# The softmax shift row of a decoder layer carried by DMA instead of by TensorE, and a reordered start of the cross-attention

## The chip, the cores and the metric

The kernel runs on one core of one Trainium2 chip. The metric is the device time of one execution in microseconds. Before the change it is 1358.77 us, the median of 3 runs (1357.2 to 1359.16).

## What is computed

One decoder layer for 8 batches of 512 tokens, width 256, in float32: a chunked linear attention with a norm, a cross-attention with 16 heads of 64 and a norm, and a feed-forward with ternary weights and a norm. The change lies in the cross-attention and in the seam before it.

```python
# first norm: x = layernorm(x + linear_attention(x))
a = einsum('bmhd,bnhd->bhmn', x @ Wq + bq, ctx @ Wk + bk) / sqrt(64)
a = where(key_mask, a, -inf)
a = softmax(a, axis=-1)
o = einsum('bhmn,bnhd->bmhd', a, ctx @ Wv + bv)
x = layernorm(x + o @ Wo + bo)
# then the feed-forward and a third norm
```

The softmax subtracts each query's maximum over the keys. The kernel adds this (negated) maximum to the scores on TensorE, before the exponential.

## The kernel before

Activations lie transposed: channels on the partitions, the 512 tokens of a batch along the free axis. The kernel has three phases that share the five instruction streams. Every wait is a semaphore written out by hand, and every engine runs its stream in order.

**The linear attention** (`linear_attention_phase`) goes through the 8 batches. Its last batch isn't finished there: its norm (`mean_last`, `square_last`, `variance_last`, `deviation_last`, `normalise`, `deviate_last`) is issued from the start of the cross-attention.

**The cross-attention** (`cross_attention_phase`) goes over 8 batches, and in each over 8 pairs of heads, `g = 8*b + p`. In pair `g`, TensorE runs, in this order: for each of 4 tiles of keys `key_scores` (three products of split values, L1253, then the row `shift` times ones, L1255, which adds the negated maximum), and behind each of them `max_scores` of pair `g+1` (L1261: queries on the partitions, so that a maximum over the keys runs along the free axis); `weighted_values` (L1276) and `sums` (L1285); `maxima_to_row(g+1)` (L1267); `keys` and `queries` of pair `g+2` (`split_matmul`, L48 to L50). Behind pair 0 and pair 4 of a batch come the output projections (`project`), behind pair 7 the values of the next batch.

The path of the maxima: VectorE's `negated_maxima` (L1118) makes, for each of 4 tiles of 128 queries and each of 2 heads, one column `nmx` of 128 partitions. `maxima_to_row` turns the columns into rows with 4 matmuls against the identity, into the PSUM bank `ROW`, and ScalarE's `shift_row` (L1004) copies that bank to the SBUF tile `shift`. ScalarE also runs the four exponentials of a pair (L977), the logarithm and exponential of a reciprocal (L990, L992), the copy of the attended values (L984), and the rounding `att_hi`, `k_hi`, `q_hi` (L1000, L1008, L1012). GpSimd adds up the probabilities (L902, L905) and splits the sums (L914 to L919).

SyncE's stream issues all loads and stores of the loop: once per batch, `store` of the batch before, `load_residual`, and `next_load` (inputs, context, masks of the next batch).

**The seam.** VectorE's order is: `finish_y_last`, `normalise(B-2)`, `queries_lo`, masks, `deviate_last`, the sums of the output weight's rows (L1204), `normalise(B-1)`, subtraction of the output weight's means (L1207), the bias, and then the first pair's maxima. TensorE's order is: values of batch 0 in three groups with `mean_last` and `variance_last` between them, then the first pair's four `max_scores`, then `maxima_to_row(0)`, then the loop. GpSimd splits the output weight (L932, L934) before its loop begins.

**The feed-forward** (`ffn_phase`) follows; the change leaves it as it is.

## Time and profile before

| | |
|---|---|
| median of 3 runs | 1358.77 us |
| the profiled execution | 1358.39 us |
| its span, first to last instruction | 1356.5 us |
| mean granted TensorE clock | 0.983 of full speed |
| TensorE busy | 1302.3 us (96%) |
| VectorE busy | 923.3 us (68%) |
| ScalarE busy | 829.8 us (61%) |
| GpSimd busy | 773.2 us (57%) |

The span and the profiled execution's own time differ by 1.9 us, which lies around the instructions. A matmul's recorded duration is longer than the distance to the next one, since they are pipelined; so the distance between starts is what TensorE's time is read from. The busy share of an engine is a mean over three phases with different limits.

### The profile page before, as it was taken

Reading aid. Unit: us, or ns where it says so; the run is one execution under the profiler, and the core shown is the slowest. Engines: PE = TensorE matmul, PEld = TensorE weight load, DVE = VectorE, ACT = ScalarE, POOL = GpSimd, SP = SyncE. Lnnn points to the kernel's source line nnn. Section 1 sums busy time; section 2 is a strip of 40 time slices with the busy share of each in tenths; the row PEclk is TensorE's granted clock in tenths of the full one; section 3 lists DMA queues with packets and bytes.
Section 4 is the critical chain, followed back from the end, with each engine's and each line's share of the span. In section 5 each row is a group of like instructions: output and inputs, shape, how many; then the busy total and the mean of one; then the engine's idle time right before and its main releaser. Section 6 shows DMA issues by size and latency. Waiting matters only on the chain.

```text
span 1356.5 us, 20922 instructions
## 1 busy us (share of the span) xinstructions
PE 1302.3 (96%) x7056; PEld 881.1 (65%) x7056; DVE 923.3 (68%) x1803; ACT 829.8 (61%) x1122; POOL 773.2 (57%) x447
## 2 busy tenths in 40 slices
PE   6999979999999999999999999999999998899995
PEld 4777756657566656666666666657666665577773
DVE  5678776674766676576657656674775678678885
ACT  2354436674766566565757665675666666678983
POOL 3504327885877687667958767694876787300000
PEclk9999989999999999999999999999999999899997
DMA  6311220000100100010010001000100100111100
GB/s 210 108 39 57 80 79 1 1 1 1 65 1 1 64 0 0 0 64 0 0 64 0 0 0 64 0 0 18 46 0 0 63 1 1 40 38 47 46 32 31
DMA packets 25535, 42.85 MB, mean 32 GB/s; under 512 B 3440, under 2 KB 7936, under 8 KB 25488
## 3 DMA queue, kind: packets, MB, share of 16 engines
q1 hardware_dynamic: 24672, 39.10, 8.5%
q0 software_dynamic: 816, 3.15, 0.7%
q8 instruction: 27, 0.44, 0.1%
q14 instruction: 20, 0.16, 0.0%
HBM read 29.66 MB, written 12.58 MB: 31 GB/s over the span
## 4 chain that ended last, share of the span: by engine, by line
PE 91%; DVE 3%; ACT 2%; POOL 2%; issue 1%; DMA 0%; POOLq 0%; SPq 0%; ACTq 0%; DVEq 0%
PE ps L1276 16%; PE ps L1253 14%; PE ps L48 11%; PE ps L50 10%; PE ps L49 10%; PE ps L1255 4%; PE ps L1261 4%; PE ps L1267 3%; PE ps L1309 2%; PE ps L1310 2%; PE ps L1308 2%; PE ps L1625 2%; PE ps L1624 2%; PE ps L1285 2%; PE ps L57 2%; PE ps L721 1%
## 5 line engine op out<-in xcount | busy, mean ns | idle before, releaser
L1118 DVE CUSTOM_DVE_ANT_0 junk<-ps,mask 128x512 bf16<-128x512 f32 x512 | 319.9, 687 | 94.2 <-PE ps L1261 92.8
L977 ACT ACTIVATE prob<-ps,mcol 128x1024 f32<-128x1024 f32 x256 | 281.8, 1116 | 138.2 <-PE ps L1255 134.9
L905 POOL TENSOR_TENSOR acc<-acc,prob 128x1024 f32<-128x1024 f32 x128 | 306.9, 2398 | 11.5
L902 POOL TENSOR_TENSOR acc<-prob 128x1024 f32<-128x1024 f32 x64 | 154.0, 2406 | 227.4 <-ACT prob L977 226.4
L1276 PE MATMUL ps<-prob,v_b 128*64 128x512 f32 x1024 | 244.5, 599 | 0.0
L919 POOL TENSOR_TENSOR acc_lo<-acc,acc_hi 128x1024 f16<-128x1024 f32 x64 | 138.8, 2169 | 5.1
L1276 PEld LDWEIGHTS ps<-prob,v_b 128*64 128x64 f32 x1024 | 67.8, 136 | 107.8 <-issue 73.9
L1253 PE MATMUL ps<-q_hi,k_hi 64*128 64x512 f32 x512 | 115.6, 446 | 4.6 <-DVE rs L226 2.8
L1261 PE MATMUL ps<-k_hi,q_hi 64*128 64x512 f32 x512 | 103.0, 398 | 6.4 <-DVE nmx L1118 5.5
L1255 PE MATMUL ps<-shift,ones_r 64*128 64x512 f32 x512 | 102.7, 395 | 0.0
L1253 PE MATMUL ps<-q_hi,k_lo 64*128 64x512 f32 x512 | 102.6, 395 | 0.0
L1253 PE MATMUL ps<-q_lo,k_hi 64*128 64x512 f32 x512 | 102.5, 395 | 0.0
L1123 DVE TENSOR_TENSOR ps<-ps,recip 128x512 f32<-128x512 f32 x64 | 44.7, 699 | 69.7 <-ACT recip L992 69.2
L984 ACT ACTIVATE pvc<-ps 128x512 f32<-128x512 f32 x64 | 38.3, 599 | 79.2 <-PE ps L1276 79.1
L1253 PEld LDWEIGHTS ps<-q_hi,k_hi 64*128 64x128 f32 x512 | 48.8, 186 | 54.7 <-issue 26.9
L1136 DVE SCALAR_TENSOR_TENSOR att_lo<-ps,bv,att_hi 128x512 fp32r<-128x512 f32 x64 | 48.0, 751 | 52.8 <-ACT att_hi L1000 52.8
L1146 DVE SCALAR_TENSOR_TENSOR q_lo<-ps,bq,q_hi 128x512 fp32r<-128x512 f32 x64 | 48.0, 751 | 39.3 <-ACT q_hi L1012 39.3
L1012 ACT ACTIVATE q_hi<-ps,bq 128x512 fp32r<-128x512 f32 x64 | 44.0, 688 | 41.8 <-PE ps L50 41.8
L1267 PEld LDWEIGHTS ps<-ident,nmx 128*128 128x128 f32 x256 | 33.9, 192 | 53.0 <-issue 53.0
L1018 ACT ACTIVATE v_b<-ps 128x512 f32<-128x512 f32 x64 | 38.2, 598 | 47.9 <-PE ps L50 47.9
L915 POOL CAST acc_hi<-acc 128x1008 f16<-128x1008 f32 x64 | 65.5, 1023 | 0.0
L1261 PEld LDWEIGHTS ps<-k_hi,q_hi 64*128 64x128 f32 x512 | 48.9, 186 | 22.0 <-DVE nmx L1118 7.1
(213 smaller groups left out, 2983.0 us busy)
## 6 DMA issues: line engine op xcount, KB each, us to landing
x_in<-in_xT SPq DMA_DIRECT2D x8, 512.0 KB, 3.7
x_scratch<-x_a SPq DMA_DIRECT2D x8, 512.0 KB, 2.9
raw<-in_cT SPq DMA_DIRECT2D x8, 512.0 KB, 5.7
raw<-x_scratch SPq DMA_DIRECT2D x8, 512.0 KB, 4.9
y<-x_scratch SPq DMA_DIRECT2D x8, 512.0 KB, 3.8
y_scratch<-y SPq DMA_DIRECT2D x8, 512.0 KB, 2.8
y_c<-y_scratch SPq DMA_DIRECT2D x8, 512.0 KB, 4.1
outT<-x SPq DMA_DIRECT2D x8, 512.0 KB, 2.8
```

The costliest lines, as they stand in the source:

```text
L48: pe.matmul(out, lh, rh, start=(i == 0), stop=False)
L49: pe.matmul(out, lh, rl, start=False, stop=False)
L50: mm = pe.matmul(out, ll, rh, start=False, stop=(i == n - 1))
L902: pool.tensor_tensor(total, prob[:, 0], prob[:, 1], ALU.add).then_inc(acc_out, 1)
L905: pool.tensor_tensor(total, total, prob[:, kt], ALU.add).then_inc(acc_out, 1)
L919: pool.tensor_tensor(acc_lo[:], acc[:], acc_hi[:], ALU.subtract).then_inc(sum_lo_out, 1)
L977: act.activation(prob[:, i].rearrange("p h t -> p (h t)"), SCORE[i % 2].rearrange("p h t -> p (h t)"), ACT.Exp, scale=SCALE, bias=mcol[:, ...
L1118: dve.tensor_tensor_reduce(junk[:, t % 2, h], SMAX[t % 2][:, h], mask[:], -1.0, -LOWEST, ALU.add, ALU.min, nmx[:, t, h * DH:h * DH + 1]).t ...
L1253: pe.matmul(banks[:, h], l[OWN[h], par, cols], r[OWN[h], par], start=(n == 0), stop=False)
L1255: mm = pe.matmul(banks[:, h], ones_r[OWN[h], :], shift[OWN[h], :], start=False, stop=True)
L1261: mm = pe.matmul(SMAX[t % 2][:, h], q_hi[OWN[h], par, toks], k_hi[OWN[h], par], start=True, stop=True)
L1276: mm = pe.matmul(PV[OWN[h], :], v[:, kt, cols], prob[:, kt, h, :], start=(kt == 0), stop=(kt == NT - 1))
```

## The change

The first group of edits concerns the maxima's path, in every pair. `maxima_to_row`, `shift_row`, the identity and the bank `ROW` go. `nmx` shrinks to one column per tile and head, doubled by the parity of the pair, and `shift` is doubled as well. SyncE issues 8 DMAs per pair, each from 128 partitions x 4 bytes of `nmx` to 512 contiguous bytes in one partition of `shift`, as soon as the two maxima of a tile are there. TensorE waits for the maxima where `maxima_to_row` stood (the banks that `queries` writes hold scores), and for the DMAs just ahead of the shift's matmuls in the first key tile. SyncE's other loads and stores are spread over the pairs of a batch.

The second group concerns the seam. The first pair's `max_scores` stand among the values and use the banks of the first keys and queries; VectorE takes the first maxima ahead of the last norm, and the output weight's means behind both. The norm's last step is cut in two functions, `root` and `scale_x1`, with the queries' low part between them for batch B-2. GpSimd splits the output weight in two halves, behind pairs 1 and 4 of batch 0, and clears `shift` before its loop.

```diff
+        def maxima_to_rows(g, p):
+            for t in range(NT):
+                sp.wait_ge(nm_out, 8 * g + 2 * t + 2)
+                for h in range(2):
+                    row = shift[h * DH:h * DH + 1, p % 2, t * P:(t + 1) * P]
+                    sp.dma_start(f32(row), f32(nmx[:, p % 2, t, h:h + 1])).then_inc(row_in[p % 2], 16)
+        def batch(b, first, last):
+            for p in range(PAIRS):
+                if not (last and p == PAIRS - 1):
+                    maxima_to_rows(per_pair(b, p) + 1, p + 1)
+                if p == 0 and not last:
+                    load_context(b + 1)
+                if p == 1 and not first:
+                    store(b - 1)
+                if p == 2 and not first:
+                    load_residual(b)
+                if p == 3 and not last:
+                    load_inputs(b + 1)
+                if p == 4 and not last:
+                    next_masks(b + 1)
...
-        def shift_row(g):
-            act.wait_ge(row_ps, g + 1)
-            act.activation(shift[:], ROW, ACT.Copy).then_inc(row_out, 1)
...
-        values_out(0, (0, 1, 2), FIRST_VAL)
+        values_out(0, (0, 1), FIRST_VAL)
         la.square_last()
-        values_out(0, (3, 4, 5), FIRST_VAL)
+        values_out(0, (2, 3, 4), FIRST_VAL)
         la.deviation_last()
-        values_out(0, (6, 7), FIRST_VAL)
-        shift_row(0)
+        values_out(0, (5, 6, 7), FIRST_VAL)
...
         la.finish_y_last()
-        la.normalise(B - 2)
+        la.root(B - 2)
         for g in range(2):
             queries_lo(g, g, FIRST_QUERY[g])
+        la.scale_x1(B - 2)
         prepare_mask(0, True)
         prepare_mask_columns(0, True)
-        la.deviate_last()
+        dve.wait_ge(bo_ps, 1)
+        dve.tensor_tensor(bo[:], ...)
+        la.subtract_mean_last()
+        first_maxima(0)
+        la.sum_squares_last()
+        for t in range(1, NT):
+            first_maxima(t)
+        la.root(B - 1)
+        la.scale_x1(B - 1)
         dve.tensor_reduce(wo_sum[:], wo[:], AX.X, ALU.add).then_inc(wo_centred, 1)
-        la.normalise(B - 1)
         dve.scalar_tensor_tensor(out=wo[:], ...)
-        negated_maxima(0, 0, 0)
         batch(0, True, False)
...
             for n, (l, r) in enumerate(((k_hi, q_hi), (k_lo, q_hi), (k_hi, q_lo))):
                 for h in range(2):
                     pe.matmul(banks[:, h], l[OWN[h], par, cols], r[OWN[h], par], start=(n == 0), stop=False)
+            if kt == 0:
+                pe.wait_ge(row_in[par], 16 * NT * (g - par) + 32 * NT)
             for h in range(2):
-                mm = pe.matmul(banks[:, h], ones_r[OWN[h], :], shift[OWN[h], :], start=False, stop=True)
+                mm = pe.matmul(banks[:, h], ones_r[OWN[h], :], shift[OWN[h], par], start=False, stop=True)
...
-        def maxima_to_row(g):
-            pe.wait_ge(nm_out, 8 * g + 8)
-            for t in range(NT):
-                mm = pe.matmul(ROW[:, t * P:(t + 1) * P], nmx[:, t, :], c["ident"][:], start=True, stop=True)
-            mm.then_inc(row_ps, 1)
...
                 if nxt:
-                    maxima_to_row(g + 1)
+                    pe.wait_ge(nm_out, 8 * g + 16)
...
+        first_max_scores(0)
+        la.mean_last()
         values(0, (0, 1), FIRST_VAL)
-        la.mean_last()
-        values(0, (2, 3, 4), FIRST_VAL)
+        first_max_scores(1)
+        values(0, (2, 3), FIRST_VAL)
         la.variance_last()
-        values(0, (5, 6, 7), FIRST_VAL)
-        for t in range(NT):
-            max_scores(0, 0, t)
-        maxima_to_row(0)
+        values(0, (4,), FIRST_VAL)
+        first_max_scores(2)
+        values(0, (5,), FIRST_VAL)
+        first_max_scores(3)
+        values(0, (6,), FIRST_VAL)
+        values(0, (7,), FIRST_VAL)
+        pe.wait_ge(la.rs_out, 2 * B - 1)
         batch(0, True, False)
```

## Rows read from the trace of the kernel before

**Rows 1.** The page: the chain that ended last, by engine and by line.
```profile
PE 91%; DVE 3%; ACT 2%; POOL 2%; issue 1%; DMA 0%; POOLq 0%; SPq 0%; ACTq 0%; DVEq 0%
PE ps L1276 16%; PE ps L1253 14%; PE ps L48 11%; PE ps L50 10%; PE ps L49 10%; PE ps L1255 4%; PE ps L1261 4%; PE ps L1267 3%; PE ps L1309 2%; PE ps L1310 2%; PE ps L1308 2%; PE ps L1625 2%; PE ps L1624 2%; PE ps L1285 2%; PE ps L57 2%; PE ps L721 1%
```

**Rows 2.** Groups of instructions: shapes, count | busy us, mean ns | idle before.
```profile
L902 POOL TENSOR_TENSOR acc<-prob 128x1024 f32<-128x1024 f32 x64 | 154.0, 2406 | 227.4 <-ACT prob L977 226.4
...
L1004 ACT ACTIVATE shift<-ps 128x512 fp32r<-128x512 f32 x64 | 38.3, 599 | 11.2 <-PE ps L1267 11.2
```

**Rows 3.** Timeline of pair 28: start us, us, engine, line, operation [idle before].
```profile
611.33 0.39 PE L1285 MATMUL ps<-acc_lo,ones_h 128*64 128x512 f16 x2
...
611.54 2.75 PE L1276 MATMUL ps<-prob,v_b 128*64 128x512 f32 x12
...
611.74 0.08 DVE L1118 DVE_READ_ACCUMULATOR2_ANT nmx<- 128x1 fp32r x1
...
614.22 0.66 PE L1267 MATMUL ps<-ident,nmx 128*128 128x128 f32 x4
...
614.72 0.45 PE L48 MATMUL ps<-bc_hi,wk_hi 128*128 128x512 f32 x1
...
615.41 0.68 ACT L1000 ACTIVATE att_hi<-ps,bv 128x512 fp32r<-128x512 f32 x1
...
617.44 2.16 POOL L919 TENSOR_TENSOR acc_lo<-acc,acc_hi 128x1024 f16<-128x1024 f32 x1
...
617.62 0.50 PE L1253 MATMUL ps<-q_hi,k_hi 64*128 64x512 f32 x2
...
617.73 0.69 ACT L1012 ACTIVATE q_hi<-ps,bq 128x512 fp32r<-128x512 f32 x1 [0.67 <-PE ps L50]
...
618.42 0.39 PE L1255 MATMUL ps<-shift,ones_r 64*128 64x512 f32 x2
```

**Rows 4.** Chain that ended last, in order of time: the values of successive pairs.
```profile
624.15 2.57 PE ps L1276 x12
...
641.98 2.58 PE ps L1276 x12
...
666.82 2.58 PE ps L1276 x12
...
690.27 2.58 PE ps L1276 x12
```

**Rows 5.** DMAs: duration on SyncE's queue (ns), issue to landing, SyncE's timeline.
```profile
L853 SPq DMA_DIRECT2D mcol_u<-in_mask_cols x8: 345/364/599, 161.8 to 950.2; - x8
...
DMA to landing us min/median/max: 2.9/5.0/5.7
...
7.53 5.30 SPq L350 DMA_DIRECT2D bT<-in_fast_bT  x1
```

**Rows 6.** Timeline of the seam and of pair 0.
```profile
191.04 0.39 PE L50 MATMUL ps<-wv_hi,bc_lo 128*128 128x512 f32 x1
...
191.29 0.75 DVE L560 SCALAR_TENSOR_TENSOR rs_a<-ps,eps,inv_a 128x512 f32<-128x512 f32 x1 [3.07 <-ACT inv_a L454]
...
193.94 2.28 DVE L1207 SCALAR_TENSOR_TENSOR wo<-wo_sum,wo 128x2048 f32<-128x2048 f32 x1
...
198.26 4.52 POOL L934 TENSOR_TENSOR wo_lo<-wo,wo_hi 128x2048 fp32r<-128x2048 f32 x1
...
203.31 0.79 PE L1253 MATMUL ps<-q_hi,k_hi 64*128 64x512 f32 x2 [0.78 <-ACT shift L1004]
...
204.73 0.66 PE L1255 MATMUL ps<-shift,ones_r 64*128 64x512 f32 x2
...
210.28 3.65 PE L1276 MATMUL ps<-prob,v_b 128*64 128x512 f32 x16
...
214.37 0.45 PE L48 MATMUL ps<-bc_hi,wk_hi 128*128 128x512 f32 x1
```

**Rows 7.** A window of the seam: length, busy us by engine, granted clock, DMA share, GB/s.
```profile
196.00:200.00 4.00, 1.59 (x4) 0.57 (x4) 3.97 (x15) 0.00 (x0) 3.63 (x2) 0.50 0.95 264
```

More of the change, by code:

```diff
@@ L89, in decoder_layer @@
         c["ones_w"] = sb(whole, "ones_w", [P, P], F32)
-        c["ident"] = sb(whole, "ident", [P, P], F32R)
         c["eps"] = sb(whole, "eps", [P, 1], F32)
@@ L374, in _, with store_x1 @@
         sp.dma_start(c["raw"][:, 0], batch_cols(x1_dram, 0)).then_inc(raw_in, 16)
[L376 to L381 removed]
+        def store_x1(b):
+            sp.wait_ge(x1_out, b + 1)
+            sp.dma_start(batch_cols(x1_dram, b), x1[:]).then_inc(stored, 16)
+        la.store_x1 = store_x1
     @block.gpsimd
@@ L806, in cross_attention_phase @@
     junk = sb(ctx, "junk", [P, 2, 2, T], BF16)
-    shift = sb(ctx, "shift", [P, T], F32R)
-    sb(ctx, "spare", [P, DK, T], F32)
+    shift = sb(ctx, "shift", [P, 2, T], F32R)
+    sb(ctx, "spare", [P, T + 2 * P], F32)
     v = sb(ctx, "v_b", [P, NT, HD], F32)
@@ L871, in load_residual, with load_norm @@
             sp.dma_start(y2[:], batch_cols(x1_dram, b)).then_inc(res_in, 16)
+        def load_norm(b):
+            sp.wait_ge(stored, 16 * b + 16)
+            sp.dma_start(f.y2[:, b], batch_cols(y2_dram, b)).then_inc(f.y_in[b], 16)
+        def maxima_to_rows(g, p):
[8 more added lines that the diff above has]
+                    maxima_to_rows(per_pair(b, p) + 1, p + 1)
+                if p == 0 and last:
+                    sp.wait_ge(x_split, B)
+                    sp.wait_ge(c_split, B)
+                    load_norm(0)
+                if p == 0 and not last:
[4 more added lines that the diff above has]
+                    load_residual(b)
+                if p == 3 and last:
+                    load_norm(1)
+                if p == 3 and not last:
+                    load_inputs(b + 1)
+                if p == 4 and not last:
+                    next_masks(b + 1)
         sp.wait_ge(la.f_step, 3 * DK + DK)
         load_masks(0)
-        la.store_last()
-        sp.wait_ge(la.qm_ps, 2 * B)
+        la.store_x1(B - 2)
+        sp.wait_ge(consts, 3)
+        maxima_to_rows(0, 0)
+        la.store_x1(B - 1)
         load_residual(0)
         sp.wait_ge(la.stored, 16 * B)
-        next_load(1)
+        batch(0, True, False)
         with sp.Fori(1, B - 1) as b:
-            store(b - 1)
-            load_residual(b)
-            next_load(b + 1)
-        store(B - 2)
-        load_residual(B - 1)
-        sp.wait_ge(x_split, B)
-        sp.wait_ge(c_split, B)
-        sp.wait_ge(stored, 32)
-        for b in range(2):
-            sp.dma_start(f.y2[:, b], batch_cols(y2_dram, b)).then_inc(f.y_in[b], 16)
+            batch(b, False, False)
+        batch(B - 1, False, True)
         store(B - 1)
@@ L927, in split_c, with split_output_weight @@
             pool.tensor_tensor(c_lo[:], raw_c, f32(c_hi[:]), ALU.subtract).then_inc(c_split, 1)
-        def split_output_weight():
+        def split_output_weight(half):
+            rows = slice(half * HALF, half * HALF + HALF)
             pool.wait_ge(wo_centred, 2)
-            pool.wait_ge(la.y_out, 2 * B)
-            pool.tensor_copy(wo_hi[:], wo[:]).then_inc(wo_split, 1)
-            pool.wait_ge(wo_split, 1)
-            pool.tensor_tensor(wo_lo[:], wo[:], f32(wo_hi[:]), ALU.subtract).then_inc(wo_split, 1)
+            pool.tensor_copy(wo_hi[:, rows], wo[:, rows]).then_inc(wo_split, 1)
+            pool.wait_ge(wo_split, 2 * half + 1)
+            pool.tensor_tensor(wo_lo[:, rows], wo[:, rows], f32(wo_hi[:, rows]), ALU.subtract).then_inc(wo_split, 1)
         def batch(b, first, last):
@@ L945, in batch @@
                 low_sums(g)
+                if first and p in (1, HALF):
+                    split_output_weight(p // HALF)
                 if p == PAIRS - 3 and not last:
@@ L959, in _ @@
         split_x(0)
-        split_output_weight()
+        pool.wait_ge(la.gate_used, B)
+        pool.memset(f32(shift[:]), 0.0).then_inc(consts, 1)
         batch(0, True, False)
@@ L1118, in negated_maxima, with first_maxima @@
                     dve.tensor_tensor_reduce(junk[:, t % 2, h], SMAX[t % 2][:, h], mask[:], -1.0, -LOWEST, ALU.add,
-                                             ALU.min, nmx[:, t, h * DH:h * DH + 1]).then_inc(nm_out, 1)
+                                             ALU.min, nmx[:, p % 2, t, h:h + 1]).then_inc(nm_out, 1)
+        def first_maxima(t):
+            dve.wait_ge(smax_ps, t + 1)
+            for h in range(2):
+                dve.tensor_tensor_reduce(junk[:, t % 2, h], FIRST_SMAX[t % 2][h], mask[:], -1.0, -LOWEST, ALU.add,
+                                         ALU.min, nmx[:, 0, t, h:h + 1]).then_inc(nm_out, 1)
         def reciprocal(g):
@@ L1253, in key_scores, with first_max_scores @@
                     pe.matmul(banks[:, h], l[OWN[h], par, cols], r[OWN[h], par], start=(n == 0), stop=False)
+            if kt == 0:
+                pe.wait_ge(row_in[par], 16 * NT * (g - par) + 32 * NT)
             for h in range(2):
-                mm = pe.matmul(banks[:, h], ones_r[OWN[h], :], shift[OWN[h], :], start=False, stop=True)
+                mm = pe.matmul(banks[:, h], ones_r[OWN[h], :], shift[OWN[h], par], start=False, stop=True)
             mm.then_inc(st_ps, 1)
+        def first_max_scores(t):
+            toks = slice(t * P, (t + 1) * P)
+            for h in range(2):
+                mm = pe.matmul(FIRST_SMAX[t % 2][h], q_hi[OWN[h], 0, toks], k_hi[OWN[h], 0], start=True, stop=True)
+            mm.then_inc(smax_ps, 1)
         def max_scores(g, p, t):
@@ L1299, in project @@
             if first:
-                pe.wait_ge(wo_split, 2)
+                pe.wait_ge(wo_split, 2 * half + 2)
             pe.wait_ge(att_out, PAIRS * b + HALF * half + HALF - 1)
```

67 lines of the change are left out of this document (28 added, 39 removed).

## Prediction

> **What bounds the kernel now.** I read the chain that ended last first. 91% of it is TensorE, and the lines of the loop carry it; L1267, the four matmuls that turn the maxima into a row, has 3% of its own [rows 1]. So TensorE's order is the spine, and an instruction taken out of it is worth its distance on that spine, unless something else then comes late. Next the timeline of one plain pair. Two plain pairs, from values to values, take 24.84 us, so one takes 12.42 us [rows 4]. The starts of its matmuls follow each other with hardly a gap. ScalarE and VectorE follow TensorE: `q_hi` starts after 0.67 us of waiting for it [rows 3]. GpSimd waits 227.4 us in all for the first exponentials [rows 2], and its last sum, done at 619.60, is used by the L1285 that follows the one at 611.33 by a pair, at 623.75: a margin of 4.1 us [rows 3]. Last the seam, the one stretch in the middle of the kernel where TensorE isn't dense: values end at 191.3, `key_scores` starts at 203.31, and in between the granted clock has fallen to the lower of its two levels, 1.2 GHz [rows 6, 7].
>
> **The loop: what goes.** The group of 12 value matmuls starts at 611.54 and lasts 2.75 us, the last of them 0.39 us like its neighbours, so the last one starts at 613.90; the first L1267 comes at 614.22, and the first L48 at 614.72 [rows 3]. With L1267 gone, the keys can take its place at 614.22: 0.50 us saved. The values go at (2.75 - 0.39) / 11 = 0.21 us a matmul and L1267 comes 0.32 us behind the last; if that extra 0.1 us goes too, it is 0.6 us. This is bounded from above, since the two kinds of matmul that then meet never meet in this trace; I take 0.50, as the wait for the maxima still stands between them, as it stands ahead of L1267 now. Pairs 2 to 62 have this pattern, 61 times: 30.5 us, at most 36.6. A lower end of zero has no reason of its own beyond the third rival, below. (Pair 0 and 1 are in the seam's sum. In front of pair 63 no keys follow, and TensorE waits for the second norm; I count nothing.) The ScalarE copy, 64 times 0.60 us [rows 2], is off the path: it takes part in no wait of TensorE except in the seam and ahead of pair 63. I cost its removal at nothing.
>
> **What is late next.** Once TensorE is 0.50 us earlier at the keys, ScalarE's chain must hold. `att_hi` starts at 615.41 and doesn't depend on L1267 but on the sums of the pair before, so it doesn't move by more than the 0.1 us for which the row's copy held it. It ends near 616.0; `k_hi` (0.69 us) ends at 616.7, and `q_hi` would be ready for its input at 617.23, half a microsecond later [rows 3]. So TensorE still leads, with 0.5 us to spare. GpSimd's margin shrinks from 4.1 to 3.6 us. The gain stands.
>
> **The loop: what comes, and who waits.** SyncE issues 8 DMAs a pair. An issue of the same shape of data (128 pieces of 4 bytes, the mask's columns) holds SyncE 0.36 us [rows 5], with the step to the next some 0.5 us, so 4 us a pair of 11.9. The two maxima of a tile come every 1.2 us or more (8 in some 5 us) and take two issues, 1.0 us: SyncE keeps up, barely. The last maximum of pair 28 is read at 611.82, and the row is first used at 618.42, which becomes 617.92 [rows 3]: 6.1 us. The last of the two issues starts some 0.6 us after the maximum. So the row is in time if it lands within 5.5 us of its issue. The nearest row: those mask columns land in 2.9 us at best, 5.0 in the median and 5.7 at worst, and there they stand right behind two loads of 512 KB [rows 5], while the last row DMA of a pair has nothing ahead of it but its sisters. I take 2.9 us, the undisturbed end, which leaves 2.6 us; the other end, 5.7, costs 0.2 us in a plain pair. No row shows a transfer from SBUF to one partition of SBUF; below 2.9 nothing is gained, since the wait is then met anyway. Behind the waiting SyncE stand the loads and stores of the batch. Each is now issued behind the maxima of its pair: the context in pair 0 for a use in pair 5, the residual in pair 2 for pair 4, the inputs in pair 3 for pair 6; at 12 us a pair each has 20 us or more. They cost nothing. The store in pair 1 waits for the projection of pair 0, done by then. The new wait of TensorE has the other three key tiles, and so all exponentials, behind it.
>
> **The seam.** Before, the last norm and the output weight's means end at 196.2 and the maxima follow, so that the row is used at 204.73 [rows 6]. After, I lay the streams out anew. TensorE's values end at 191.3 before; four score steps of some 0.33 us stand ahead of that end: 192.6. The fourth step stands ahead of two values (6 matmuls of 0.23 us each, 2.8 us together), so it ends at 189.8. VectorE takes its two maxima by 191.2, and SyncE issues by 191.8 and the row lands at 194.7 with 2.9 us. So the row is used 10.0 us earlier. But then VectorE has the norm (2.7 us, from 191.2 to 193.9) and twice 2.3 us of output weight (L1207; the reduction over the same tensor taken as long) [rows 6] before it can serve pair 1: 198.6. TensorE stops ahead of pair 1's third score tile until two tiles' first maxima are there, 199.9, then has 1.5 us of scores and the 3.6 us of values as at 210.28, and reaches the keys at 205.1. Before, that was 214.37: 9.3 us, with the L1267 in it. The bounds: if the stops of 1.4 and 2.4 us bring the clock down again, TensorE's 8.7 us of matmuls in pair 0 take up to twice as long, partly under VectorE's work: 4 us less; if everything fits tighter, 10.5. GpSimd's splitting of the output weight moves from a stretch in which it had nothing else into pairs 1 and 4. The subtraction takes 4.52 us for the whole tensor [rows 6], 2.3 for a half, and the copy, which I take at half of that, brings 3.4 us a half: inside the margin of 3.6. With a copy as slow as the subtraction, pair 2 would wait 0.9 us, once.
>
> **The sum.** 30.5 + 9.3 = 39.8 us. The profiled execution took 1358.39 us, of which 1356.5 are the span, so its own forecast is 1318.6; the median of the runs lies 0.4 us above it: 1319.0 us.
>
> **Rivals.** First, the row lands too late (the slower side). If a DMA of 128 four-byte pieces into one partition takes L us instead of 2.9, every plain pair waits L - 5.5 us, and 39 of the pairs are plain; behind the projections a pair lasts 17.8 us and behind the values 23.5 [rows 4], which covers it. At L = 6.5 the whole gain is eaten; at 8.0 the kernel takes 1358.8 - 39.8 + 39 x 2.5 = 1416 us. For it: nothing in the trace shows this shape, and one issue took 5.30 us on SyncE, with a dozen loads outstanding [rows 5]. Against it: the mask columns, as many and as small pieces, landed in 5.7 us behind 1 MB. I give it 8 in 100, and 6 in 100 to a landing between 5.5 and 6.5 us, with times from 1320 to 1358.
>
> Of this the Trainium skill's page "DMA: Bandwidth & Descriptors" (Rules for kernel authors) warns: a last dimension that isn't contiguous becomes one descriptor per element, and a plain DMA with a rearranged access pattern is put at 19 times a hardware transpose. By that rule the shift would be the bottleneck and this rival the case; the mask columns' row speaks for the contrary at 512 bytes in all.
>
> Second, the seam gives little: the row is late or the clock stays at 1.2 GHz through pair 0. Then the seam brings 3 us, the sum 33.5, the time 1325. For it: before, the clock was at 0.50 between 196 and 200, with TensorE busy 1.59 us of 4 [rows 7]. 12 in 100.
>
> Third, another engine takes half of each 0.50 us, since ScalarE has just 0.5 us to spare; it may also be less by itself if the meeting of values and keys costs more than the one that goes. 61 x 0.25 = 15 us less gain: 1334. Against it: the chain laid out above. 8 in 100.
>
> Fourth, nothing measurable: the DMAs' stalls happen to balance. 2 in 100.
>
> **How the numbers follow.** The forecast has 64 in 100; its own range, from the unknown 30.5 to 36.6 us and the seam's 5.3 to 10.5 us, is 1312 to 1323. The range over all reaches to the third rival and no further, 1310 to 1335, and leaves the two cases of a late row out, about 2 in 10. A measurement of this kernel can't tell less than some 0.2% (2.7 us) from no change. Faster: forecast, second and third rival, and most of the half-late row, 0.88; same 0.04; slower 0.08.
>
> **What would show it.** In the trace after, a plain pair takes 11.92 us (11.82 with the 0.6), the keys start 0.3 us behind the last value matmul, and the first L1255 of a pair's scores follows the first six matmuls without idle time. If the first rival holds, that idle time stands there and names the DMA. The row DMAs' landing is under 5.5 us, and SyncE issues each within a microsecond of its maxima. `q_hi` still waits for TensorE. The first `key_scores` starts near 192.6, its row lands near 194.7, and the keys behind pair 0 start near 205, with a granted clock of 1.00. The prediction is wrong if the landing is over 5.5 us, if an engine other than TensorE sets the plain pair, or if the clock drops in the seam.

## The result, and the profile after

The changed kernel takes 1324.14 us (median of 4 runs, 1323.08 to 1327.98). The kernel before took 1357.99 us beside it (4 runs, 1356.68 to 1359.16). The ratio is 0.9757, with a 95% interval from 0.974 to 0.9774: 2.4% faster. The profiled execution took 1323.5 us, with a span of 1321.6 us, 34.9 us less than the span before. The forecast was 1319.0, with a range from 1310 to 1335.

The page of the changed kernel: the busy time of each engine, the DMA packets, the chain by line, and the row DMAs' landing. The chain answers [rows 1]; of [rows 2], GpSimd's wait for the first exponentials is now 219.7 us, and the copy into `shift` is no longer there.

```profile
PE 1270.6 (96%) x6800; PEld 846.9 (64%) x6800; DVE 923.3 (70%) x1802; ACT 792.9 (60%) x1058; POOL 776.1 (59%) x449
...
DMA packets 99118, 43.07 MB, mean 33 GB/s; under 512 B 77152, under 2 KB 81520, under 8 KB 99072
...
PE ps L1310 16%; PE ps L1285 14%; PE ps L48 11%; PE ps L50 10%; PE ps L49 10%; PE ps L1301 4%; PE ps L1289 4%; PE ps L1342 2%; PE ps L1344 2%; PE ps L1343 2%; PE ps L1660 2%; PE ps L1661 2%; PE ps L1319 2%; POOL acc L931 2%; PE ps L716 1%
...
shift<-nmx SPq DMA_DIRECT2D x512, 0.5 KB, 2.0
```

TensorE still carries the chain. The 3% of the row's matmuls (L1267 before) are gone, and no DMA line is in their place: all that DMAs and SyncE have in the chain lies in the first 21 us, at the loads of the start. In the new numbering L1310 is `weighted_values`, L1319 `sums`, L1285 `key_scores`, L1289 the shift's matmuls, L1301 `max_scores`, L1139 the maxima (L1145 those of the first pair), and L883 the row DMAs.

The timeline of a plain pair of the changed kernel, from the values to the sums of the next pair. It answers [rows 3]. Columns: start, duration, engine, line, operation, idle time before.

```profile
592.69 2.75 PE L1310 MATMUL ps<-prob,v_b 128*64 128x512 f32 x12
...
592.88 0.08 DVE L1139 DVE_READ_ACCUMULATOR2_ANT nmx<- 128x1 fp32r x1
...
595.36 0.50 PE L48 MATMUL ps<-bc_hi,wk_hi 128*128 128x512 f32 x1
...
595.70 0.40 PE L49 MATMUL ps<-bc_lo,wk_hi 128*128 128x512 f32 x1
...
596.46 0.69 ACT L1028 ACTIVATE att_hi<-ps,bv 128x512 fp32r<-128x512 f32 x1 [0.39 <-DVE ps L1158]
...
598.29 0.50 PE L1285 MATMUL ps<-q_hi,k_hi 64*128 64x512 f32 x2
...
598.40 0.69 ACT L1036 ACTIVATE q_hi<-ps,bq 128x512 fp32r<-128x512 f32 x1 [0.67 <-PE ps L50]
598.58 2.15 POOL L945 TENSOR_TENSOR acc_lo<-acc,acc_hi 128x1024 f16<-128x1024 f32 x1
...
599.10 0.39 PE L1289 MATMUL ps<-shift,ones_r 64*128 64x512 f32 x2
...
601.23 4.98 SPq L883 DMA_DIRECT2D shift<-nmx  x8
...
604.43 0.39 PE L1319 MATMUL ps<-acc_lo,ones_h 128*64 128x512 f16 x2
```

The keys (L48) now stand where L1267 stood, 2.67 us behind the start of the values. The shift's matmuls (L1289) follow 0.81 us behind the first `key_scores` (598.29 to 599.10), 0.80 us before [rows 3], and name no DMA. `q_hi` still waits 0.67 us for TensorE. GpSimd's `acc_lo` ends at 600.73 and the sums that use it start at 604.43, 3.7 us later. A plain pair from values to values, in the chain of the changed kernel, answering [rows 4]:

```profile
592.86 2.58 PE ps L1310 x12
604.82 2.58 PE ps L1310 x12
```

The distance is 11.96 us. From the start of one pair's `key_scores` to the next pair's, the median of the 38 plain pairs that keys follow is 11.98 us, against 12.42 us before: 0.44 us less.

The seam of the changed kernel, answering [rows 6]:

```profile
191.20 0.08 DVE L1145 DVE_READ_ACCUMULATOR2_ANT nmx<- 128x1 fp32r x1
191.20 0.75 DVE L555 SCALAR_TENSOR_TENSOR rs_a<-ps,eps,inv_a 128x512 f32<-128x512 f32 x1
191.31 1.12 SPq L883 DMA_DIRECT2D shift<-nmx  x2
...
192.84 0.50 PE L1285 MATMUL ps<-q_hi,k_hi 64*128 64x512 f32 x2
...
193.85 2.28 DVE L1242 TENSOR_REDUCE wo_sum<-wo 128x8 f32<-128x2048 f32 x1
193.90 0.50 PE L1289 MATMUL ps<-shift,ones_r 64*128 64x512 f32 x2
...
196.16 2.29 DVE L1244 SCALAR_TENSOR_TENSOR wo<-wo_sum,wo 128x2048 f32<-128x2048 f32 x1
...
196.80 3.87 POOL L928 TENSOR_TENSOR acc<-prob 128x1024 f32<-128x1024 f32 x1 [27.13 <-ACT prob L1005]
...
199.73 0.62 PE L1301 MATMUL ps<-k_hi,q_hi 64*128 64x512 f32 x2 [2.92 <-DVE nmx L1139]
...
202.41 4.11 PE L1310 MATMUL ps<-prob,v_b 128*64 128x512 f32 x16
...
206.45 0.50 PE L48 MATMUL ps<-bc_hi,wk_hi 128*128 128x512 f32 x1
```

Windows of it, answering [rows 7] (length, busy time and count of PE, PEld, DVE, ACT and POOL, granted clock, DMA share, GB/s):

```profile
200.00:204.00 4.00, 4.00 (x18) 1.98 (x18) 3.43 (x12) 1.12 (x1) 3.71 (x3) 0.58 0.10 1
204.00:208.00 4.00, 4.00 (x19) 1.85 (x16) 0.00 (x0) 0.60 (x1) 3.84 (x4) 1.00 0.47 126
```

The row is used 10.8 us earlier than before and the keys behind pair 0 start 7.9 us earlier. In between TensorE stops 2.92 us for the maxima of pair 1, which stand behind the output weight's two instructions on VectorE, and then the clock is at its lower level (1.2 GHz): the mean is 0.58 of full speed in the first window. Half speed for 3.4 of the 4 us gives that mean ((1 - 0.58) x 4 / 0.5).

**Where the 34.9 us come from.** I compare the start of the first `key_scores` of pair g in both traces: the lead of the changed kernel. Pair 1 is the one at 209.41 after and 217.25 before; the last point ahead of everything that the change touches on TensorE's path is the matmul of the output bias, which starts at 178.14 before and 177.09 after.

| stretch | lead at its end | gained there | forecast |
|---|---|---|---|
| start to output bias | 1.05 | 1.05 | 0 |
| seam, to pair 1 | 7.84 | 6.8 | 9.3 |
| pair 1 to pair 62 (the 61 key groups) | 33.71 | 25.9 | 30.5 |
| pair 62 to the loop's last sums | 33.72 | 0.0 | 0 |
| to the end | 34.93 | 1.2 | 0 |

The first row is scatter. In the runs below the lead at the output bias lies between -3.2 and +1.3 us, and +1.3 us belongs to a kernel that keeps the identity and `ROW`. So a single time of one kernel is uncertain by some 2 us from this alone, and I compare leads below, each less its own lead at the output bias ("corrected").

The last row isn't the change's either. Ahead of pair 63 the lead rises to 34.97 us, but it is back at 33.71 at that pair's second key tile, and at 33.72 at the last sums (1164.47 before, 1130.75 after). Behind them the granted clock differs. The windows are the same stretch of work, before and then after:

```profile
1164.00:1174.00 10.00, 9.53 (x29) 7.02 (x29) 5.53 (x8) 7.72 (x14) 0.42 (x1) 0.67 0.00 0
```

```profile
1130.00:1140.00 10.00, 9.25 (x32) 7.01 (x33) 5.52 (x8) 8.52 (x15) 0.70 (x1) 0.83 0.00 0
```

By the same working as for the seam, that is about 6.6 us at the lower level before and 3.4 us after. In the runs below the gain from the last sums to the end goes with the clock there and not with the row's way: `e3_one_dma`, `e7_seam_undone` and `e9_copy_kept` have the row DMAs and the long fall, and gain 0.0 to 0.2 us; the seven runs with a fall of 3.4 us gain 1.1 to 1.4. `e2_late_half` and `e8_seam_alone`, whose fall begins earlier and lasts 10 us, gain 0.5 and 0.4.

### The profile page after: what moved, and what is told of

The parts are those of the page before. It is cut to its first block, busy times and chain, and to the rows that moved or that the text cites. A ratio compares the mean times of both kernels' runs of the same rounds, so it can differ in the third digit from the quotient of the medians.

```text
span 1321.6 us, 21020 instructions
## 1 busy us (share of the span) xinstructions
PE 1270.6 (96%) x6800; PEld 846.9 (64%) x6800; DVE 923.3 (70%) x1802; ACT 792.9 (60%) x1058; POOL 776.1 (59%) x449
## 2 busy tenths in 40 slices
DMA packets 99118, 43.07 MB, mean 33 GB/s; under 512 B 77152, under 2 KB 81520, under 8 KB 99072
## 4 chain that ended last, share of the span: by engine, by line
PE 89%; POOL 3%; DVE 3%; ACT 2%; issue 1%; SPq 1%; DMA 1%; POOLq 0%; ACTq 0%; DVEq 0%
PE ps L1310 16%; PE ps L1285 14%; PE ps L48 11%; PE ps L50 10%; PE ps L49 10%; PE ps L1301 4%; PE ps L1289 4%; PE ps L1342 2%; PE ps L1344 2%; PE ps L1343 2%; PE ps L1660 2%; PE ps L1661 2%; PE ps L1319 2%; POOL acc L931 2%; PE ps L716 1%
## 5 line engine op out<-in xcount | busy, mean ns | idle before, releaser
L1139 DVE CUSTOM_DVE_ANT_0 junk<-ps,mask 128x512 bf16<-128x512 f32 x504 | 314.9, 686 | 89.1 <-PE ps L1301 87.8
L931 POOL TENSOR_TENSOR acc<-acc,prob 128x1024 f32<-128x1024 f32 x128 | 306.9, 2398 | 11.5
L928 POOL TENSOR_TENSOR acc<-prob 128x1024 f32<-128x1024 f32 x64 | 155.3, 2426 | 219.7 <-ACT prob L1005 218.4
L1310 PE MATMUL ps<-prob,v_b 128*64 128x512 f32 x1024 | 245.0, 599 | 0.2 <-ACT prob L1005 0.2
L1310 PEld LDWEIGHTS ps<-prob,v_b 128*64 128x64 f32 x1024 | 67.9, 137 | 108.1 <-issue 74.9
L1285 PE MATMUL ps<-q_hi,k_hi 64*128 64x512 f32 x512 | 114.8, 444 | 4.2 <-DVE rs L225 4.0
L1301 PE MATMUL ps<-k_hi,q_hi 64*128 64x512 f32 x504 | 100.9, 395 | 3.8 <-DVE nmx L1139 3.8
L1289 PE MATMUL ps<-shift,ones_r 64*128 64x512 f32 x512 | 102.1, 394 | 0.1
L1285 PE MATMUL ps<-q_lo,k_hi 64*128 64x512 f32 x512 | 102.1, 394 | 0.0
L1285 PE MATMUL ps<-q_hi,k_lo 64*128 64x512 f32 x512 | 102.0, 394 | 0.0
L1285 PEld LDWEIGHTS ps<-q_hi,k_hi 64*128 64x128 f32 x512 | 48.2, 184 | 55.3 <-issue 27.0
L1028 ACT ACTIVATE att_hi<-ps,bv 128x512 fp32r<-128x512 f32 x64 | 44.1, 689 | 33.8 <-DVE ps L1158 33.8
L1301 PEld LDWEIGHTS ps<-k_hi,q_hi 64*128 64x128 f32 x504 | 47.7, 185 | 19.1 <-DVE nmx L1139 4.9
```

Of the source, the lines that this page charges most:

```text
L928: pool.tensor_tensor(total, prob[:, 0], prob[:, 1], ALU.add).then_inc(acc_out, 1)
L931: pool.tensor_tensor(total, total, prob[:, kt], ALU.add).then_inc(acc_out, 1)
L1139: dve.tensor_tensor_reduce(junk[:, t % 2, h], SMAX[t % 2][:, h], mask[:], -1.0, -LOWEST, ALU.add, ALU.min, nmx[:, p % 2, t, h:h + 1]).then ...
L1285: pe.matmul(banks[:, h], l[OWN[h], par, cols], r[OWN[h], par], start=(n == 0), stop=False)
L1289: mm = pe.matmul(banks[:, h], ones_r[OWN[h], :], shift[OWN[h], par], start=False, stop=True)
L1301: mm = pe.matmul(SMAX[t % 2][:, h], q_hi[OWN[h], par, toks], k_hi[OWN[h], par], start=True, stop=True)
```

## The experiments

**The seam alone, and the rows alone.** First the two groups of edits were taken apart. `e8_seam_alone` is the kernel before with the second group only; the row still goes by L1267 and ScalarE's copy.

```diff
+        la.subtract_mean_last()
+        first_maxima(0)
+        la.sum_squares_last()
+        for t in range(1, NT):
+            first_maxima(t)
+        la.root(B - 1)
+        la.scale_x1(B - 1)
         dve.tensor_reduce(wo_sum[:], wo[:], AX.X, ALU.add).then_inc(wo_centred, 1)
-        la.normalise(B - 1)
...
         shift_row(0)
```

> The kernel before with the new seam, the rows still by matmuls and ScalarE's copy. Theory: only the seam's 7 us come, 1351 us, with plain pairs of 12.42 us and the first score matmul near 193 us instead of 203. Rival, the seam gives nothing without the DMA: 1357 us.

Measured: 1350.63 us (1348.96 to 1352.69), ratio 0.995 (0.9933 to 0.9966). The corrected lead is 6.5 us at pair 1 and 6.3 at pair 62; a plain pair takes 12.42 us. `e7_seam_undone` is the complement: the rows by DMA, with the seam as before.

```diff
-        first_maxima(0)
         la.sum_squares_last()
-        for t in range(1, NT):
-            first_maxima(t)
+        dve.tensor_reduce(wo_sum[:], wo[:], AX.X, ALU.add).then_inc(wo_centred, 1)
         la.root(B - 1)
         la.scale_x1(B - 1)
-        dve.tensor_reduce(wo_sum[:], wo[:], AX.X, ALU.add).then_inc(wo_centred, 1)
...
+        negated_maxima(0, 0, 0)
```

> The changed kernel with the seam in its old order (values, last norm, output weight, then the first pair's maxima in their old banks), the rows still by DMA. Theory: the loop's gain and the seam's gain add up. In the changed kernel's trace the loop took 0.44 us less per pair; so this kernel keeps 61 x 0.44 = 27 us plus 1 us at the last pair, and gives the seam's 7 us back: 1330 us, with plain pairs of 11.97 us and a first use of a row near 204 us. Rival, the seam's gain is a difference of the start-up alone or is given back in pair 0: 1324 us, as the changed kernel.

Measured: 1332.19 us (1330.5 to 1332.27), ratio 0.9808 (0.9792 to 0.9824). Its corrected lead at pair 1 is -0.1 us, at pair 62 it is 25.6 us, and a plain pair takes 11.98 us. So the two groups add up to within 1 us: 6.3 and 25.6 make 31.9, and the whole change has 32.7 at the same point. The seam's order is worth nothing in the loop. What the row's way is worth in the old seam isn't clear: the first `key_scores` of `e7_seam_undone` start 1.8 us ahead (corrected), and that is gone by pair 1, but the granted clock between 208 and 212 was 0.89 there and 1.00 before. The 1 us that I expected at the last pair isn't there: its lead at the end is 25.6 us, as at pair 62.

**Is the row's landing near the edge?** The first rival was a row that lands too late. `e1_late_all` issues all 8 DMAs only when all 8 maxima are there.

```diff
-                sp.wait_ge(nm_out, 8 * g + 2 * t + 2)
+                sp.wait_ge(nm_out, 8 * g + 8)
```

> The changed kernel with one edit: SyncE issues a pair's 8 row DMAs only when all 8 maxima are there. The eighth issue then starts some 4.5 us behind the last maximum (7 steps of 0.64 us), and lands 2.0 us later, at 6.6 us, where the row is used 6.15 us behind the maximum. Theory of the slack (the row has to be there 6.1 us behind the last maximum, or every plain pair waits for the rest): 39 plain pairs x 0.4 us = 18 us slower than the changed kernel, 1342 us, and the trace shows TensorE waiting for the DMA ahead of the shift's matmuls. Rival, there is more slack than the plain pair shows: 1324 us.

Measured: 1344.9 us (one run), a plain pair of 12.37 us. Its timeline:

```profile
605.31 0.08 DVE L1139 DVE_READ_ACCUMULATOR2_ANT nmx<- 128x1 fp32r x1
...
605.42 4.98 SPq L883 DMA_DIRECT2D shift<-nmx  x8
...
610.75 0.50 PE L1285 MATMUL ps<-q_hi,k_hi 64*128 64x512 f32 x2
...
611.84 0.50 PE L1289 MATMUL ps<-shift,ones_r 64*128 64x512 f32 x2
```

and what the shift's instructions waited for in it, over the whole kernel (us in total, times; weight loads and matmuls are counted each for itself, so this is more than TensorE lost):

```profile
  DMA shift<-nmx: 47.5, 71
```

The last of eight issues starts some 4.4 us behind the first (4.98 less one of 0.60), at 609.8, and lands 2.0 us later, at 611.8: there L1289 starts, 0.3 us later than it would without the wait. A pair loses 0.39 us, so another 0.1 us goes behind the wait. This is the first rival made real: the mechanism decides exactly where it was placed, and the changed kernel stays clear of it because the issues are spread behind their tiles. `e2_late_half` moves only the last four.

```diff
-                sp.wait_ge(nm_out, 8 * g + 2 * t + 2)
+                sp.wait_ge(nm_out, 8 * g + (2 * t + 2 if t < 2 else 8))
```

> The changed kernel with the last four row DMAs of a pair issued only when all 8 maxima are there. The last issue starts some 2 us behind the last maximum and lands at 4 us, 2 us before it is used. Theory of the slack: no change, 1324 us, plain pairs of 11.97 us. If the DMAs' queueing on SyncE were itself on the path, this would be 1 to 2 us a pair slower, 1365 us or more.

Measured: 1323.59 us (one run), a plain pair of 11.98 us. The last issue now starts 1.8 us behind the last maximum instead of 0.7 (medians), and those 1.1 us cost nothing, which fits the margin worked out below. In its seam TensorE waits 1.35 us for the first row, and then 1.66 us for the maxima of pair 1, 1.3 us less than in the changed kernel, so that this is hidden too.

**Do the DMAs cost anything beside the landing?** `e3_one_dma` issues one of the eight; seven eighths of the shift row are left out.

```diff
-            for t in range(NT):
+            for t in (NT - 1,):
...
-                for h in range(2):
+                for h in (1,):
...
-                pe.wait_ge(row_in[par], 16 * NT * (g - par) + 32 * NT)
+                pe.wait_ge(row_in[par], 8 * (g - par) + 16)
```

> Of the eight row DMAs of a pair only the last one (fourth tile, second head) is issued; seven eighths of the shift row are left out, so the exponentials are taken with a wrong maximum there. Theory (the eight DMAs and SyncE's 5 us a pair lie wholly beside TensorE's stream): plain pair 11.98 us, whole kernel 1324 us, the same as with eight. Rival (the 35,000 or more small packets or SyncE's issues slow the streams, by memory traffic or by late loads): a plain pair shorter by 0.05 us or more, whole kernel 1321 us or less.

Measured: 1326.76 us (one run); the plain pair is 11.98 us, and the lead grows by 25.8 us from pair 1 to pair 62, as in the changed kernel (25.9). The packets fall from 99118 to 34605, and nothing on TensorE's path in the loop moves. The time is 3.3 us longer than that of the changed kernel's profiled execution, for three reasons outside the loop: the corrected lead at pair 1 is 1.2 us smaller (the clock, below), the start took 1.0 us longer, and the gain behind the last sums is 1.0 us smaller (the clock again).

**Was the copy worth nothing?** `e9_copy_kept` puts a copy of the same size back on ScalarE; it writes a spare tile.

```diff
+                if nxt:
+                    act.activation(spare[:, :T], c["wfc"][:, 0, :T], ACT.Copy)
```

> The changed kernel with a ScalarE copy of 128x512 put back where the row's copy stood, from a constant into a spare tile that nothing reads: 63 times 0.6 us of ScalarE, nothing else. Theory (the copy was off the path, as the prediction costed it): plain pair 11.98 to 12.0 us, whole kernel 1324 us. Rival (with TensorE 0.44 us faster a pair, ScalarE has no 0.6 us to spare): q_hi no longer waits for TensorE but TensorE for q_hi or for an exponential, a plain pair 0.1 to 0.5 us longer, 1328 to 1345 us.

Measured: 1330.03 us (one run), yet the plain pair is 11.97 us and the lead grows by 25.8 us from pair 1 to pair 62, again as without the copy. ScalarE's timeline in it:

```profile
601.56 0.62 ACT L1073 ACTIVATE spare<-wfc 128x512 f32<-128x512 f32 x1
...
602.08 0.68 ACT L1028 ACTIVATE att_hi<-ps,bv 128x512 fp32r<-128x512 f32 x1
...
604.01 0.69 ACT L1036 ACTIVATE q_hi<-ps,bq 128x512 fp32r<-128x512 f32 x1 [0.67 <-PE ps L50]
```

The copy fills the 0.39 us for which `att_hi` waited for VectorE, and `q_hi` waits for TensorE as long as before. In the loop ScalarE's time for it is worth nothing, as costed. This copy isn't on the row's way, though: nothing waits for it, so the run tests ScalarE's time and not the row's. The whole is 6.5 us longer than the changed kernel's profiled execution, and almost all of that lies outside the loop: the lead at the output bias is -3.2 instead of 1.05 us (4.2 us), where no copy runs, the clock in the seam takes 1.3 us, and the gain behind the last sums is 1.0 us smaller. I take the 1330.03 for no statement on the copy.

**Why 0.44 us and not 0.50?** In the changed kernel L48 starts 0.31 us behind the last value matmul (592.69 + 2.36 = 595.05), and L49 0.34 us behind L48, where it was 0.29 before. Two theories: the gap belongs to TensorE, when one kind of matmul follows the other; or it is the wait for the maxima between them. `e4_wait_early` moves that wait ahead of the last four values.

```diff
                 pe.wait_ge(exp_out, 4 * g + 4)
+                if nxt:
+                    pe.wait_ge(nm_out, 8 * g + 16)
                 weighted_values(g, p, (3,))
...
-                if nxt:
-                    pe.wait_ge(nm_out, 8 * g + 16)
```

> The changed kernel with TensorE's wait for a pair's last maxima moved from between the values and the keys to ahead of the values' last key tile (the maxima are there 1 us earlier still). The loop gained 0.44 us a pair instead of the 0.50 forecast, and the first key matmul stands 0.31 us behind the last value matmul and 0.34 ahead of the next, where 0.21 and 0.23 are usual. Theory A: that 0.2 us is TensorE's own, from the change of the kind of matmul; then nothing changes, 1324 us. Theory B: the wait between them holds the weights' load back; then up to 62 x 0.2 us = 12 us come, 1312 us.

Measured: 1324.48 us (1322.9 to 1325.16), ratio 0.9755 (0.9739 to 0.9772), a plain pair of 11.97 us. The changed kernel run again in the same series (`e0_after_again`) gave 1325.53 us (1324.4 to 1327.21), ratio 0.9763 (0.9747 to 0.978): no difference.

> The changed kernel, unaltered, as the yardstick for the next three on the same chip: 1324 us, plain pairs of 11.98 us.

The timeline of `e4_wait_early`:

```profile
604.15 2.75 PE L1310 MATMUL ps<-prob,v_b 128*64 128x512 f32 x12
606.83 0.50 PE L48 MATMUL ps<-bc_hi,wk_hi 128*128 128x512 f32 x1
607.16 0.39 PE L49 MATMUL ps<-bc_lo,wk_hi 128*128 128x512 f32 x1
```

With nothing to wait for, L48 still stands 0.32 us behind the last value matmul (606.51) and L49 0.33 us behind L48. The two gaps are TensorE's own. That they come from the change of the matmuls' shape (128 x 64 to 128 x 128) is argued, not shown.

**What the clock costs in the seam.** Six kernels whose seam differs in small things only (the time of the rows, the place of a wait, the copy) ran with and without a fall of the granted clock, which gives its price. At the start of pair 0 all six have the same corrected lead, 9.4 to 9.5 us; they part between there and pair 1. The half-clock time is worked out from three windows (200 to 212) as above.

| kernel | granted clock 200:204, 204:208 | us at half clock | corrected lead at pair 1 |
|---|---|---|---|
| e4_wait_early | 1.00, 1.00 | 0 | 8.3 |
| e2_late_half | 1.00, 1.00 | 0 | 8.3 |
| e0_after_again | 0.66, 0.91 | 3.4 | 7.1 |
| changed kernel | 0.58, 1.00 | 3.4 | 6.8 |
| e3_one_dma | 0.50, 0.66 | 6.8 | 5.6 |
| e9_copy_kept | 0.91, 0.50 (then 0.74 in 208:212) | 6.8 | 5.5 |

So each 3.4 us at the lower level cost about 1.4 us. In `e4_wait_early` the stop ahead of it is as long and the clock stays up; in `e2_late_half` the stop is in two parts, 1.35 and 1.66 us. The end of the stop in `e4_wait_early`, to be set beside the 2.92 us of the changed kernel:

```profile
200.75 0.50 PE L1301 MATMUL ps<-k_hi,q_hi 64*128 64x512 f32 x2 [2.94 <-DVE nmx L1139]
```

A matmul of this form takes 0.50 us right behind the stop at full clock and 0.62 us in the changed kernel. `e1_late_all` and `e8_seam_alone` fell for 3.4 us as well, so of eight traces with a stop there, two show no fall.

**Taking the stop away.** If the stop comes from the output weight standing ahead of pair 1's maxima, moving it behind them should give the rest. `e5_wo_later`:

```diff
                     negated_maxima(bn, g + 1, pn)
+                if first and p == 0:
+                    centre_weight()
...
         la.scale_x1(B - 1)
-        dve.tensor_reduce(wo_sum[:], wo[:], AX.X, ALU.add).then_inc(wo_centred, 1)
-        dve.wait_ge(wo_centred, 1)
-        dve.scalar_tensor_tensor(out=wo[:], ...)
```

> The changed kernel with VectorE's work on the output weight (the sums and the subtraction, 4.6 us) moved from ahead of pair 1's maxima to behind them. The trace of the changed kernel shows TensorE stopped for 2.9 us in pair 0 for those maxima, and the clock at its lower level for 3.4 us right behind; the lead over the kernel before falls from 10.5 us at pair 0 to 7.8 at pair 1. Theory: the stop is the output weight's, and 2.6 us come back: 1321.5 us, with no clock drop in the seam. Rival: VectorE is then late with the keys' low part of pair 2, and the time stays 1324.

Measured: 1322.36 us (1319.98 to 1323.34), ratio 0.9734 (0.9717 to 0.975). The stop is gone and the clock stays at 1.00. The corrected lead is 11.5 us at pair 1, but 10.7 at pair 2: something takes 0.8 us back. Its timeline:

```profile
201.87 4.92 POOL L931 TENSOR_TENSOR acc<-acc,prob 128x1024 f32<-128x1024 f32 x2
...
202.21 2.28 DVE L1177 TENSOR_REDUCE wo_sum<-wo 128x8 f32<-128x2048 f32 x1
...
204.53 4.41 DVE L1179 SCALAR_TENSOR_TENSOR wo<-wo_sum,wo 128x2048 f32<-128x2048 f32 x1
...
206.87 2.15 POOL L940 TENSOR_TENSOR acc_hi<-acc,ones_w 128x16 f16<-128x16 f32 x1
...
208.86 0.74 DVE L1168 SCALAR_TENSOR_TENSOR k_lo<-ps,bk,k_hi 128x512 fp32r<-128x512 f32 x1
...
209.65 0.50 PE L1289 MATMUL ps<-q_hi,k_hi 64*128 64x512 f32 x2 [0.98 <-DVE k_lo L1168]
```

The subtraction takes 4.41 us instead of 2.29. Behind it stands `k_lo` of pair 2, which reads the bank that pair 1's second key tile writes, so TensorE waits for it. `e6_wo_later_wait_early` joins this to the earlier wait.

> The edits of the two runs before this one together. By the theories as they stand (the wait gives nothing, the output weight 2.6 us): 1321.5 us. If the wait gives 12 us: 1309.5.

Measured: 1321.92 us (1321.62 to 1322.53), ratio 0.9736 (0.972 to 0.9752); the corrected lead at pair 2 is 10.8 us, as in `e5_wo_later`. The earlier wait brings nothing here either. `e10_wo_halves` cuts the subtraction in two, the second half in pair 4.

```diff
+                if first and p == 0:
+                    sum_weight()
+                    centre_weight(0)
...
+                if first and p == HALF:
+                    centre_weight(1)
...
-            pool.wait_ge(wo_centred, 2)
+            pool.wait_ge(wo_centred, half + 2)
```

> As the version with VectorE's output weight work behind pair 1's maxima (1322.36 us, ratio 0.9734), but the subtraction of the means is cut in two halves: the first behind pair 1's maxima, the second in pair 4, and GpSimd splits each half behind its own subtraction. Theory (in that version the 4.4 us subtraction beside GpSimd delays the low parts of pair 1 and costs 0.8 to 1.0 us there): the stop of 0.98 us goes, the lead over the kernel before rises by 0.4 us from pair 1 to pair 2 instead of falling by 0.8, kernel at 1321.3 us, ratio about 0.9727. Rival (a half costs as much waiting as the whole, or the second half is late in pair 4): the same 1322.4 us or more, with a stop in pair 1 or 5.

Measured: 1321.07 us (1319.13 to 1323.15), ratio 0.9729 (0.971 to 0.9747). The corrected lead is 11.5 us at pair 1 and 11.8 at pair 2, against 6.8 and 7.2 in the changed kernel, so the 0.8 us are no longer given back. Of the 4.5 us at pair 2, 1.5 are the clock's: without the fall the kernels of the table have 8.7 us there, and the stop itself is worth 3.

```profile
203.56 3.35 DVE L1182 SCALAR_TENSOR_TENSOR wo<-wo_sum,wo 128x1024 f32<-128x1024 f32 x1
...
206.83 0.74 DVE L1168 SCALAR_TENSOR_TENSOR k_lo<-ps,bk,k_hi 128x512 fp32r<-128x512 f32 x1
```

The half still takes 3.35 us beside GpSimd, but `k_lo` starts at 206.83, 2.0 us earlier than in `e5_wo_later`. In the times the step from the changed kernel (0.9757 and 0.9763) to this one (0.9729) isn't resolved, since the intervals touch; the leads show 4.5 us at pair 2. Its median is the lowest of the kernels here, and not to be told from those of the two versions before it.

## Why the prediction was right, point by point

**TensorE's order as the spine: right.** The loop's gain is TensorE's, a plain pair at a time, and it is alike in the long pairs.

**0.50 us a pair, 30.5 us: right in kind, mis-sized.** Measured 0.44 us, 25.9 us over the loop. The 0.50 was the distance from L1267 to L48, with the next matmul as before. The keys did take L1267's place (0.31 us behind the last value matmul against a forecast 0.3), but the matmul behind them now stands 0.34 us away instead of 0.29. The other bound, 0.60, counted on keys at the values' pace of 0.21 us, and that gap is TensorE's own: `e4_wait_early` shows that the wait for the maxima, which I gave as the reason for 0.50, has no part in it. What goes missing is what the third rival says in its second half, that the new meeting of matmuls costs more than the one that goes; it costs 0.06 us a pair, and not 0.25. 61 x 0.06 is 3.7 of the 4.6 us. Two pairs hold most of the rest: pair 7 gained 0.16 us (why isn't shown), and pair 59 0.01 us. In pair 59 TensorE waits for VectorE's maxima ahead of a `max_scores`, 0.42 us before and 0.85 us after, so there VectorE takes the whole gain. It is the first half of the third rival, in one pair of 61. The line in the trace of the changed kernel:

```profile
1061.40 0.50 PE L1301 MATMUL ps<-k_hi,q_hi 64*128 64x512 f32 x2 [0.85 <-DVE nmx L1139]
```

**What is late next: right.** `q_hi` waits 0.67 us for TensorE as before; GpSimd's margin is 3.7 us (forecast 3.6).

**The row lands in time: right, with two sizes off that offset each other.** From the last maximum to the row's first use it is 6.15 us in the median (forecast 6.1). The landing takes 2.0 us, where I took 2.9. An issue holds SyncE longer than the mask columns' did:

```profile
L883 SPq DMA_DIRECT2D shift<-nmx x512: 468/600/1639, 182.8 to 1106.4; - x171
...
  DMA shift<-nmx: 0.5, 1
...
DMA to landing us min/median/max: 1.9/2.0/3.3
```

These lines are what the trace of the changed kernel says of the tile `shift`: duration on SyncE's queue in ns, what the readers waited for, and the landing. With a step of 0.63 us the eight issues take 5.0 us of SyncE's 12 (forecast 4), and the last starts some 0.7 us behind the last maximum. It lands at 2.7 us, so the margin is 3.4 us; forecast, 2.6. `e2_late_half` used 1.1 us of it and lost nothing; `e1_late_all` used 3.7 and lost 0.3. Both agree with that number. One wait of 0.5 us is left, in pair 0. The Trainium skill, page "DMA: Bandwidth & Descriptors" (section on the anatomy of one DMA), puts the fixed part of a DMA at about 2.0 us, for DMAs that GpSimd issues. These are issued by SyncE, and their 2.0 us are the same number; no run here takes the 2.0 us apart. Its factor of 19, weighed in the prediction, compares with a hardware transpose, which no run here has. What the prediction drew from it, that the shift would be the bottleneck, didn't happen.

**The copy and GpSimd's split at nothing: right.** `e9_copy_kept` shows the first for the loop, and pair 63, below, for its one wait at the end. The split of a half took 3.4 us as forecast, and left no stop in pair 2.

**The seam, 9.3 us: right in its order, mis-sized by the clock and by the score steps.** Measured 6.8 us. VectorE ran as laid out: the norm from 191.20 (191.2), the two instructions on the output weight from 193.85, and it was free at 198.4 (198.6). TensorE started again at 199.73 (199.9), and the row was used at 193.90 (194.7). What failed first is the last term, "1.5 us of scores and the 3.6 us of values": they took 6.7 us, from 199.73 to 206.45, since the clock had fallen. That is 1.5 us, and the bound "4 us less" covered it. The other 1.0 us is that VectorE's chain wasn't ahead though this execution was 1.05 us ahead at the output bias. TensorE had lost that: from the output bias to the last value matmul it took 12.90 us before (178.14 to 191.04) and 15.43 after (177.09 to 192.52), so the four score steps among the values cost 2.5 us, where the prediction laid out 1.3, four times 0.33. Each took 0.6 us on average, with the loop's gaps at both ends: at the fourth, 0.32 us ahead of it, and 0.34 us from the first value matmul behind it to the next. Where the clock stayed up, nearly the same code has 8.3 us. So the second rival holds in its mechanism (the clock falls) but not in its size (3 us). The prediction had named a fall of the clock in the seam as a sign that it is wrong, and forecast a granted clock of 1.00 there; on that point it was wrong. The fall cost 1.5 us, where the rival gave it 6.

**Pair 63 at nothing: right, though it looks wrong at first.** The first and second key tile of pair 63 in the trace of the kernel before, and then in that of the changed kernel:

```profile
1144.19 0.50 PE L1253 MATMUL ps<-q_hi,k_hi 64*128 64x512 f32 x2 [0.78 <-ACT shift L1004]
...
1148.16 0.80 PE L1253 MATMUL ps<-q_hi,k_hi 64*128 64x512 f32 x2 [2.78 <-DVE rs L226]
```

```profile
1109.22 0.50 PE L1285 MATMUL ps<-q_hi,k_hi 64*128 64x512 f32 x2
...
1114.45 0.58 PE L1285 MATMUL ps<-q_hi,k_hi 64*128 64x512 f32 x2 [4.03 <-DVE rs L225]
```

Before, the first tile waited 0.78 us for ScalarE's copy of the row, since no keys stood between to cover it. That wait and L1267 are gone, and the first tile comes 1.26 us earlier. But TensorE does wait for the second norm (`rs`), one tile later than the prediction places it, and now 1.25 us longer: 4.03 us for 2.78. From tile to tile the lead is back at 33.71 us, so the row's way is worth nothing there. Who reads only the start of a pair books 1.3 us that the next wait takes back.

**The sum.** 39.8 forecast; -4.6 (loop), -2.5 (seam), +1.2 (the clock behind the last sums) and +1.05 (start) give 34.9, and 34.9 were measured. The last two are luck: 2.3 us of this execution's gain aren't the change's. Of the rivals, a part of the second is seen, and small parts of the third.

## What to carry to other kernels

A small transpose on the path of the bounding engine can go by DMAs of a few hundred bytes, if their use is some 3 us behind the last issue and the issues are spread over the time in which the pieces come up; count the issue time of all pieces, not only the landing. An instruction taken out between two kinds of matmul gave back less than its distance on TensorE (0.44 of 0.50 us), and one put in between cost more (0.6 for 0.33 us): each change between the kinds showed its gap. Where an order is laid out anew, price a stop of TensorE twice: the stop, and the time at half clock that can follow it. And follow a lead to the next wait before booking it: what one wait gives, the next can take.

## What the runs showed of the hardware

A transfer of 128 pieces of 4 bytes from 128 partitions into one partition landed in 2.0 us in the median (1.9 to 3.3), while its issue held SyncE 0.60 us, more than the 0.36 us of the mask columns [rows 5] that have as many pieces. In `e3_one_dma`, with one such DMA a pair, the issue took 0.47 us in the median. 64,500 more packets a run cost TensorE nothing.

VectorE and GpSimd held each other up in whole instructions. In `e5_wo_later` the subtraction starts at 204.53 beside L931, which ends at 206.79, and ends itself at 208.94, 2.15 us after that: about its time alone (2.29). GpSimd's L940, 0.22 us elsewhere, lasts from 206.87 until 209.02. The reduction ahead of it, beside the same pair of L931, took its usual 2.28 us. In the changed kernel the subtraction (196.16 to 198.45) came first, and GpSimd's L928 took 3.87 us instead of 2.4, ending 2.2 us behind it. The Trainium skill, page "SBUF — State Buffer" (Who interferes with whom), says this: a VectorE instruction with two SBUF inputs and a GpSimd instruction that reads SBUF exclude each other for the whole instruction, whoever starts first, and a reduction never contends. All four cases agree.

Open: why the granted clock fell behind TensorE's stop in some executions and not in others of nearly the same code, why its fall behind the last sums lasted 3.4 us in some and twice that in others, and where the start-up's scatter of 4 us comes from.
